# Two decoder layers on one core: the local attention's score masks taken off TensorE

## The reference

```
offs = jnp.arange(-WIN, WIN + 1)                       # WIN = 16
kidx = qpos[:, None] + offs[None, :]
valid = (kidx >= 1) & (kidx < s)                       # s = 256
scores = jnp.einsum('bqhd,bqwhd->bhqw', Q * scale, Kw) # 16 heads of 8 dimensions
scores = jnp.where(valid[None, None, :, :], scores, -1e+30)
attn = jax.nn.softmax(scores, axis=-1)
ctx = jnp.einsum('bhqw,bqwhd->bqhd', attn, Vw)
```

## Time and profile before

| | |
|---|---|
| median of 3 runs | 572.17 us (571.77 to 574.89) |
| profiled execution, its own time | 577.35 us |
| its span, first to last instruction | 575.5 us |
| PE busy over the span | 480.7 us (84%) |
| DVE, ACT, POOL busy | 376.9, 223.1, 191.9 us |
| LOCAL heads (slots 38 to 101) | 50.9 to about 129 us of the span |

### The profile page before, as it was taken

One profiled execution on the slowest core, in us unless ns is written; L12 is line 12 of the kernel. 1 busy time (PEld: TensorE's weight loads), 2 busy tenths in 40 slices (PEclk: granted clock), 3 DMA queues, 4 the chain that ended last, 5 costly groups with the idle time before them and its releaser, 6 DMA issues. The chain is left out here.

```text
span 575.5 us, 10505 instructions
## 1 busy us (share of the span) xinstructions
PE 480.7 (84%) x3778; PEld 235.1 (41%) x3824; DVE 376.9 (66%) x923; ACT 223.1 (39%) x451; POOL 191.9 (33%) x326
## 2 busy tenths in 40 slices
PE   3899899988988879885369998697799888999993
PEld 2435344433433334332126985255323333444441
DVE  7545675776768668648995455844478885376574
ACT  1312345444664755663002113232214666624220
POOL 7641637466338363260600007600432200000000
PEclk9989899988999999998589998889599999999997
DMA  7221202144443210005212040000211100260700
GB/s 238 64 59 45 58 2 65 48 135 130 135 121 97 56 32 26 3 2 197 96 48 102 2 166 1 1 1 0 72 50 53 50 2 3 61 160 1 220 18 19
DMA packets 27091, 38.03 MB, mean 66 GB/s; under 512 B 3792, under 2 KB 19728, under 8 KB 26656
## 3 DMA queue, kind: packets, MB, share of 16 engines
q1 hardware_dynamic: 27040, 37.36, 21.6%
HBM read 23.91 MB, written 0.59 MB: 43 GB/s over the span
## 5 line engine op out<-in xcount | busy, mean ns | idle before, releaser
L1096 DVE TENSOR_REDUCE nmax<-bank 128x2 f32<-128x512 f32 (+2 forms) x240 | 144.6, 624 | 85.6 <-PE bank L865 39.9
L977 ACT ACTIVATE arena<-bank 128x512 f32<-128x512 f32 (+2 forms) x256 | 131.0, 526 | 124.4 <-PE bank L869 85.9
L865 PE MATMUL bank<-arena 62*128 62x256 bf16 (+2 forms) x512 | 86.9, 259 | 11.9 <-DVE nmax L1096 6.6
L507 PE MATMUL bank<-causal_qk,identb 128*128 128x512 bf16 x233 | 74.4, 417 | 17.3 <-DVEq L1480 7.2
L869 PE MATMUL bank<-arena 64*128 64x256 bf16 (+2 forms) x512 | 86.2, 257 | 2.2 <-ACT arena L977 1.5
L910 PE MATMUL bank<-arena 128*32 128x256 f32 (+4 forms) x1088 | 73.1, 348 | 9.4 <-ACT arena L977 3.1
L865 PEld LDWEIGHTS bank<-arena 62*128 62x128 bf16 x512 | 29.9, 94 | 79.9 <-issue 49.9
L507 PEld LDWEIGHTS bank<-causal_qk,identb 128*128 128x128 bf16 x275 | 24.3, 106 | 47.9 <-issue 13.7
L732 POOL TENSOR_SCALAR_AFFINE_SELECT arena<-arena 128x256 f32<-128x256 f32 x64 | 25.6, 409 | 50.2 <-ACT arena L977 49.4
L869 PEld LDWEIGHTS bank<-arena 64*128 64x128 bf16 x512 | 30.3, 94 | 16.7 <-issue 7.0
L691 POOL TENSOR_TENSOR arena<-qk,arena 128x512 bf16<-128x512 f32 x15 | 17.3, 1156 | 57.0 <-ACT arena L939 57.0
(11 more groups left out here) (316 smaller groups left out, 832.2 us busy)
## 6 DMA issues: line engine op xcount, KB each, us to landing
arena<-arena SPq DMA_DIRECT2D x96, 128.0 KB, 2.4
fcw<-in_fc1T SPq DMA_DIRECT2D x16, 256.0 KB, 3.5
arena<-in_fc2T SPq DMA_DIRECT2D x1, 4096.0 KB, 12.7
arena<-comb_rows SPq DMA_DIRECT2D x16, 256.0 KB, 4.6
fcw<-in_last SPq DMA_DIRECT2D x1, 2304.0 KB, 8.0
arena<-pos_rows SPq DMA_DIRECT2D x16, 128.0 KB, 3.0
arena<-comb_rows SPq DMA_DIRECT2D x16, 128.0 KB, 4.5
w<-in_w SPq DMA_DIRECT2D x1, 1216.0 KB, 5.9
```

What stands on the lines that cost most here:

```text
L507: nc.tensor.matmul(bank[:, :], m.identb[:, :], m.causal_qk[:, 0:4, :], start=True, stop=True)
L865: mins = t.matmul(mout[:, i, :], stack_rows(m, nm, h0 + i, 0, MAX_ROWS)[:, qt * P:(qt + 1) * P], stack_rows(m, nm, h0 + i, 1, MAX_ROWS)[:, ...
L977: s.activation(m.prob[h % 8][:, 0:w], score_bank(n, h)[:, 0:w], ACT.Exp).then_inc(exps, 1)
L1096: v.tensor_reduce(m.nmax[n % 2][:, qt, h0:h0 + nh], MX[c % NMX][:, 0:nh * (k1 - k0)].rearrange("p (h k) -> p h k", h=nh), AX.X, ALU.max, n ...
```

## The change

One line of the table: all heads that PE masked, and those that POOL or DVE masked, are dealt anew, even heads to DVE and odd heads to POOL.

```diff
     masked = {FULL: [], CAUSAL: [(h, "pool") for h in range(HEADS)],
-              LOCAL: [(h, ("pe", "pool", "pe", "dve")[h % 4]) for h in range(HEADS)]}
+              LOCAL: [(h, ("dve", "pool")[h % 2]) for h in range(HEADS)]}
```

## The result

| | before | changed |
|---|---|---|
| median | 572.06 us (571.77 to 574.89, 4 runs) | 586.65 us (583.84 to 588.89, 4 runs) |
| profiled execution, its own time | 577.35 us | 588.89 us |
| span, mean granted clock | 575.5 us, 0.938 | 587.2 us, 0.924 |
| PE, DVE, POOL busy | 480.7, 376.9, 191.9 us | 492.0, 384.0, 210.8 us |

The changed kernel is slower: ratio 1.0239, 95% interval 1.0197 to 1.0281, or 14.6 us between the medians. Forecast were +10 and 575 to 589 us.

What follows compares the result with a forecast made beforehand. PE paces the LOCAL stretch on average, but POOL is the bound beside its splittings. POOL 9.3 - relief 1.9 + clock 1.4 + shared side 1.5 = +10.3, rounded to +10 on 572.2: 582 us; own range 577 to 587, widened to 575 to 589.

Steps and rivals of the forecast that it cites:

- rival 3: POOL and DVE block each other and PE's clock drops at each wait: +18, 590 us; chance 14%.
- POOL's masks beside the splittings: LOCAL jobs 0, 2, 3: added masks in POOL's list delay PV group 2 by 3.14, 3.8 and 2.34: +9.3 us.
- The relief: PE in the LOCAL stretch: dropping 32 L882 can bring 4.6 us at most, of which 1.9 is realised.
- The minima: DVE in the LOCAL stretch: 16 more minima, 7.3 us busy, cost nothing on average, at most 1.8 us.
- the shared side: DVE minima lengthen POOL's runs by a quarter microsecond each, six more minima in three runs: +1.5 us, from 0 to 5.0.
- The clock: PE behind job 2's new wait: a slow-clock episode not covered by POOL's lateness, +1.4 us, from 0 to 5.9.
- one uncovered spell of 3.9 us: Job 2 gets a new low-clock episode, sized on the 3.9 us of slow matmuls after job 0's 1.04 us wait.
- From the profile to the median: Whole kernel: a difference worked out from the 577.35 us profiled execution is put on the median, 572.17 us.
- The relief winning: Rival 1: POOL's lateness falls into slack in the LOCAL stretch, 4.6 us of relief remain: 567.6 us; chance 8%.
- cancelling: Rival 2: later waits take back half of POOL's lateness, against full relief: 0 to +2, 573 us; chance 8%.
- What would show it: Changed profile: PV waits for POOL some ten times, 8 us or more; job 4's first head some 9 us later.

Runs made afterwards that it cites:

- POOL's part alone: Kernel before with heads by turns pe, pool, pe, pool: 16 more POOL masks, L882 kept, no DVE minima; 580.80 us, ratio 1.0156.
- the fillers: Changed kernel with six filler matmuls of 512 columns ahead of PE's wait at five PVs; 583.19 us, ratio 1.0219.
- the second profiles: Kernel before and changed kernel each profiled again unchanged: 574.17 us and 585.99 us.
- the first two experiments: Against the kernel before: 32 L882 removed with nothing in their place, 572.21 us; then 16 more POOL masks, L882 kept, no DVE minima, 580.80 us.

## Why the prediction came out

Sign and range were right, and so was the main cause, POOL's list; the +10 was a third too small, since the relief was put too high and the minima with the clock too low. That the time lies in the range owes something to the range's width: 586.65 is nearer to rival 3's 590 than to 582.

- **POOL's masks beside the splittings, +9.3.** Right as a mechanism: POOL's part alone measures +9.1 (580.80 against 571.68), and three selects cut to one bring all but 1 us back. That 9.1 is so near to 9.3 is in part luck, since that version also drops DVE's 16 minima and has some low clock of its own; POOL's masks doubled with the old minima kept were not run. Counted from the first L869, PV group 2 of job 0 came after 16.50 us before and comes after 19.84 now: +3.3, where I had 3.14 - 0.4 = 2.7.
- **The relief, -1.9 of 4.6.** The engine's time per matmul was read rightly, at least by span times clock (5.0 us), but as time it is 0 alone and 1.4 beside POOL's list. The assumption that failed is that work taken off PE where PE sets the pace comes out of the span. What took it back shows as the lower mean clock; why that clock is lower is open.
- **The minima, "nothing on average", and +1.5 for the shared side.** This is the term that was mis-sized most. They cost 7.2 us in the changed kernel, 5.8 with L882 kept (586.57 against 580.80), and 3.3 for 32 of them with POOL's list as before. Only 16 of the 32 are new, and no run prices those alone. The holding up of POOL that I costed is there, 2.5 us of select time, and one wait of 1.97 us for DVE that I had not, but PE's idle time in the stretch doesn't grow by them; the cost is busy time at the lower clock: the stretch has 0.86 and 0.78 with the minima, 0.93 without, 0.96 in POOL's part alone.
- **The clock, +1.4.** Too small: 13.6 us of the 97.08 (14%) and 22.5 of the 102.29 (22%) are lost to it in the two profiles, 3.4 and 1.7 before. Some is lost in waits and costs nothing; what the fillers brought back is 3.5 us by the medians. I took one uncovered spell of 3.9 us, and the first profile has two of 9 to 10 and two of 3 to 4. By job 2's PV group 2 the delay, counted from the first L869, was 65.68 - 54.90 = 10.8 us where I had 5.7. In POOL's part alone, with the clock at 0.96, it is 61.58 - 54.90 = 6.7 at the same place, so that most of my miss there goes with the minima and the clock.
- **From the profile to the median.** The profiled execution of before was slow for its kernel (577.35 against 572), the changed one's less so (588.89 against 586.65). Profile to profile it is +11.5, near the +10.3 of the sum, and +11.8 between the second profiles (585.99 and 574.17, the latter above its median too); median to median it is +14.6, and that is what the forecast has to answer to.
- **The rivals.** The relief winning or cancelling is refuted by the first two experiments. Rival 3, POOL and DVE holding each other up with the clock falling, was priced +18 at 14%. Both of its parts are seen, and the truth lies between it and the forecast.
- **What would show it.** PV's waits were seven, not ten, but 9.3 us (nine and again 9.3 in the second profile); their releaser was named as ACT or "issue"; POOL worked without a gap from 92.8 to 112.0 us; the end of the stretch came 12.3 us later, where the first head of job 4 was to come 9 later; L877 to L910 is 0.23 us (84.34 to 84.57), as it was before where no L882 stood between.

Open: why minima on DVE go with a lower clock of TensorE, while POOL's waits alone hardly do. The minima lengthen some waits (3.4 us at most against 2.2) and add waits for DVE, and that may be all: the version with three heads on DVE has no PV wait over 1.4 us, but has those of 1.67 and 1.25 us for DVE with the low clock behind them. Against it, the fall doesn't follow from the wait alone, as the two profiles with head 9 on DVE show. No version was clearly faster than the kernel before.

## What to carry to other kernels

Read a consumer's wait against the list of the engine that it waits for: an engine a third busy on average can be the bound where a long run stands ahead of what is wanted, and there a short operation more in that run is paid nearly in full. Work taken from the busiest engine is worth its start-to-start distance at most, and may be worth nothing: here the clock came out lower with the work gone. So price clock and waits together, and try filler where a wait can't be avoided; here it didn't cost time. Set a profile's difference beside a profile of the same quality, since a single execution of either kernel can be 1% off its median.

## What wasn't expected of the hardware

The granted clock over all of an execution differs with the edit and with the execution (0.941 at 573.5 us to 0.964 at 567.0 us in runs of the same kernel before), and with it the time of parts that no edit touches: the experts' part took 173.2, 174.7, 176.1, 178.0 and 178.6 us in profiles of four kernels, at clocks of 0.90, 0.88, 0.87, 0.87 and 0.86. Thirty filler matmuls (some 6.5 us of work, by the 1.3 for six) made a kernel no slower and probably faster, and 32 matmuls taken away made one no faster. A wait of 2.00 us at the same place of one kernel was followed by the full clock in one execution and by 0.54 for 7 us in the other.
